# Eight key tiles of the value sums from half-precision parts made by VectorE, on one Trainium2 core

## The reference, cut to what matters

```
B, T, D = 2, 4096, 256; 16 heads of 16
x_norm = layernorm(x) * gamma + beta
q, k = l2_normalize(heads(x_norm @ w_q)), l2_normalize(heads(x_norm @ w_k)); v = heads(x @ w_v)
align = q @ k.T                                           # per batch and head, 4096 x 4096
resonance = 0.5 + 0.5 * tanh((align - 0.27) * 15)
gate_q, gate_k = 0.25 + 0.75 * sigmoid(q . g_q), 0.25 + 0.75 * sigmoid(k . g_k)
fused = (resonance * gate_q[:, None] * gate_k[None, :]) @ v
x = layernorm(x + fused @ w_o + b_o)
h = silu(fp4_linear(x, w_gate)) * fp4_linear(x, w_up)     # hidden width 704, blocks of 16 rounded to a 4-bit grid
x = layernorm(x + fp4_linear(h, w_down))
```

## Time and profile before

| what | value |
|---|---|
| median of three runs | 4383.23 us (4379.05 to 4384.30) |
| the profiled execution's own time | 4378.88 us |
| its span | 4377.1 us |
| TensorE busy, matmuls | 4111.8 us, 94% |
| ScalarE busy | 4017.1 us, 92% |
| VectorE busy | 1561.6 us, 36% |
| GpSimd busy | 159.5 us, 4% |
| DMA | 313.7 MB, mean 72 GB/s |

### The profile page before, as it was taken

How to read it: one execution, slowest core, us unless ns; L and a number is a source line. 1 busy time by engine, 2 the same in 40 slices (tenths; PEclk the granted TensorE clock), 3 DMA queues, 4 the chain that set the end, 5 groups by cost and what they waited for, 6 DMA issues and landing times.

```text
span 4377.1 us, 69385 instructions
## 1 busy us (share of the span) xinstructions
PE 4111.8 (94%) x28776; PEld 1285.9 (29%) x28776; DVE 1561.6 (36%) x4540; ACT 4017.1 (92%) x3271; POOL 159.5 (4%) x120
## 2 busy tenths in 40 slices
PE   7988899999999999999999999999999999999997
PEld 5651222222222222222222222222222222222223
DVE  6754023333333332333233333333333333333236
ACT  4669999999999999999999999999999999999993
POOL 2330000000000000000000000000000000000001
PEclk9999999999999999999999999999999999999998
DMA  4454444344434443444334433443345334433450
GB/s 114 124 129 78 70 76 65 61 68 78 65 63 67 78 68 60 66 78 71 60 63 78 77 55 62 78 78 56 61 78 78 56 61 78 78 59 59 77 83 13
DMA packets 179871, 313.70 MB, mean 72 GB/s; under 512 B 65264, under 2 KB 141808, under 8 KB 154608
## 3 DMA queue, kind: packets, MB, share of 16 engines
q1 hardware_dynamic: 179568, 309.41, 42.1%
HBM read 266.82 MB, written 42.47 MB: 71 GB/s over the span
## 4 chain that ended last, share of the span: by engine, by line
PE 69%; ACT 23%; DVE 4%; issue 3%; DMA 1%; SPq 1%; POOL 0%; POOLq 0%; DVEq 0%; ACTq 0%
PE ps L1268 35%; ACT room L706 22%; PE ps L1258 20%; PE ps L1295 8%; PE ps L1318 4%; DMA m_f<-fused_t 1%; DVE room L858 1%; PE ps L1213 0%; DVE st L812 0%; DVE xnT L848 0%; PE ps L1224 0%; PE ps L1308 0%; DVE sm L773 0%; DVE sm L774 0%; DVE sm L775 0%
## 5 line engine op out<-in xcount | busy, mean ns | idle before, releaser
L706 ACT ACTIVATE room<-ps 128x1024 f32<-128x1024 f32 (+1 forms) x2816 | 3787.1, 1417 | 178.4 <-PE ps L1258 162.2
L1268 PE MATMUL ps<-room,vt 128*32 128x512 f32 x16384 | 2051.2, 601 | 0.0
L1258 PE MATMUL ps<-qs,room 64*128 64x512 f16 x8198 | 1325.9, 383 | 203.7 <-ACT room L706 182.6
L1258 PEld LDWEIGHTS ps<-qs,room 64*128 64x128 f16 x8198 | 310.4, 93 | 1749.5 <-ACT room L706 1123.1
L1268 PEld LDWEIGHTS ps<-room,vt 128*32 128x32 f32 x16384 | 388.1, 108 | 945.3 <-issue 945.3
L1295 PE MATMUL ps<-wguT,m_xqT 128*128 128x352 f32 x960 | 348.2, 485 | 0.0
L967 DVE TENSOR_TENSOR vz<-ps,vz 128x352 f32<-128x352 f32 x120 | 63.0, 525 | 757.7 <-ACT vz L716 757.7
L972 DVE TENSOR_TENSOR vz<-ps,vz 128x352 f32<-128x352 f32 x120 | 63.0, 525 | 595.9 <-PE ps L1295 595.9
L1318 PE MATMUL ps<-wdnT,wqk 128*128 128x256 f32 x720 | 198.9, 404 | 0.6 <-DVE wqk L937 0.6
L1295 PEld LDWEIGHTS ps<-wguT,m_xqT 128*128 128x128 f32 x960 | 162.6, 189 | 105.2 <-issue 54.3
L600 POOL TENSOR_TENSOR m_x<-m_x,bo 128x256 f32<-128x256 f32 x60 | 43.9, 731 | 3876.7 <-DMA m_x<-in_L_attn_x_dram 3876.7
(11 more groups left out here) (172 smaller groups left out, 2198.0 us busy)
## 6 DMA issues: line engine op xcount, KB each, us to landing
room<-k_parts SPq DMA_DIRECT2D x520, 256.0 KB, 9.4
vt<-v_gated SPq DMA_DIRECT2D x65, 1024.0 KB, 17.9
qs<-q_parts SPq DMA_DIRECT2D x520, 32.0 KB, 10.1
gqb<-q_gates SPq DMA_DIRECT2D x256, 64.0 KB, 2.2
...
fused_t<-fs SPq DMA_DIRECT2D x256, 32.0 KB, 1.7
...
```

The lines of the kernel that those rows point to most:

```text
L706: act.activation(res[:, c, o:o + m, :], ps[:, o:o + m, :], ACT.Sigmoid, scale=2 * SHARP / QK_UP ** 2, bias=-2 * SHARP * THRESH).then_inc(b ...
L1258: ins = pe.matmul(ps[:, BANK[n % 2] + i, :], ks[o:o + HROWS, par, h // 2, kt * P:(kt + 1) * P], qs[o:o + HROWS, par, h // 2, :], start=Tru ...
L1268: ins = pe.matmul(ps[32 * h:32 * h + 32, SUM_BANK, :], vt[:, par, n * HD:n * HD + 32], r, start=kt == 0, stop=kt == KT - 1, skip_group_che ...
```

## The change

Eight of the 32 key tiles, those with kt = 0, 3, 6, 12, 15, 18, 21 and 24, are no longer summed in full precision. VectorE writes a high and a low half-precision part of the resonances of such a tile (`split_results`, two instructions of 2048 columns, after ScalarE's group 4c) and TensorE adds eight half-precision matmuls for it (`split_sums`) at group 4c+4: the stationary operand holds 16 columns of high and 16 of low parts of the values of a head, so that the sums of a head now fill 32 rows, whose halves the output projection adds (`wo` loaded twice, four chunks for two). For this the values are brought to a known scale: stage A keeps their largest magnitude, a chain between the stages turns it into a power of two, and `scale_values` multiplies the values of each unit and makes their parts. Full-precision sums use 16 columns for 32, except key tile 1, which comes first and is padded with zeros. The sums are stored with one DMA of 256 KB for four of 32 KB and loaded with 256 KB for 128 KB; the loads of the query gates move behind them. VectorE's order in a unit interleaves the eight splits with the pieces of the tile's tail; units 0 to 3 have no splits. A unit has 18 loads for 17. The diff, cut to its core:

```diff
-NIN = 2 * 2 * len(PAIRS) + 1
+NIN = 2 * 2 * len(PAIRS) + 2
...
-        at[4 * c + 2] = [0, 1] if c == 0 else [3 * c + 1]
+        at[4 * c + 2] = [1, 0] if c == 0 else [3 * c + 1]
...
+def split_at(n):
+    return [SPLIT.index(c) for c in SPLIT if 4 * c + 4 == n]
...
+SPLIT = [0, 1, 2, 4, 5, 6, 7, 8]
...
+RES_UP = 2.0 ** 12
+V_TOP = 2.0 ** 22
+FIRST_KT = 1
+NST, NFL = 1, 1
...
+def is_split(kt):
+    return kt % 3 == 0 and kt // 3 in SPLIT
...
-WEIGHT_LOADS = 9
+WEIGHT_LOADS = 8 + 2 * HG
...
-A_CHAIN = 14
+A_CHAIN = 16
...
-    fd = nc.dram_tensor("fused_t", [B, D, T], F32).ap()
+    fd = nc.dram_tensor("fused_t", [B, 2 * D, T], F32).ap()
...
-        wo = sb("wo", [P, DC, D])
+        wo = sb("wo", [P, NG, D])
...
-        vt = sb("vt", [P, 2, KT * HG * HD + HD])
+        vt = sb("vt", [P, 2, KT * HG * HD])
...
+        vp = carve(wtmp, 64, [2, HG, 2 * HD])
...
+        vh = carve(xT[:, :, :].rearrange("p c n -> p (c n)"), 0, [2, NSPLIT, HG * 2 * HD], FP16)
...
+        r_hi = [carve(wgu_flat, 1024 * i, [HG * BLK], FP16) for i in range(2)]
+        r_lo = [carve(a, 0, [HG * BLK], FP16) for a in (wdn_flat, xnT_flat)]
...
-        m_f = sb("m_f", [P, DC, P])
+        m_f = carve(wgu_flat, 2048, [NG, P])
...
-            sp.dma_start(wo[:, :, :], rows(w_o)).then_inc(s_w, 16)
...
+            for h in range(HG):
+                for m in range(2):
+                    o = 32 * h + m * HD
+                    sp.dma_start(wo[o:o + HD], w_o.rearrange("(g h d) n -> h d g n", g=NG, h=HG)[h]).then_inc(s_w, 16)
...
+                    if n == NIN - 2:
+                        sp.dma_start(vt[:, par], vd[b, g].rearrange("p k e -> p (k e)")).then_inc(b_in[par], 16)
+                        continue
                     if n == NIN - 1:
-                        sp.dma_start(vt[:, par, 0:KT * HG * HD], vd[b, g].rearrange("p k e -> p (k e)"))\
+                        sp.dma_start(vp[:, par, :, 0:HD],
+                                     vd[b, g, :, FIRST_KT, :].rearrange("p (h d) -> p h d", d=HD))\
                           .then_inc(b_in[par], 16)
                         continue
...
-                for h in range(HG):
-                    sp.dma_start(fd[b, (g * HG + h) * HD:(g * HG + h + 1) * HD, bass.ds(i * BLK, BLK)],
-                                 fs[32 * h:32 * h + HD, :]).then_inc(b_st, 16)
...
+                sp.dma_start(fd[b, g * P:(g + 1) * P, bass.ds(i * BLK, BLK)], fs[:, :]).then_inc(b_st, 16)
...
+            def load_sums(dst, j, t, done):
...
                 b, i = j // QB, j % QB
-                return sp.dma_start(dst, fd[b, :, bass.ds(i * BLK + t * P, P)].rearrange("(c r) t -> r c t", r=P))
+                sp.dma_start(dst, fd[b, :, bass.ds(i * BLK + t * P, P)].rearrange("(g r) t -> r g t", r=P))\
+                  .then_inc(done, 16)
...
-                for h in range(HG):
-                    sp.dma_start(gqb[32 * h:32 * h + 32, :],
-                                 gqd[b, g * HG + h:g * HG + h + 1, bass.ds(i * BLK, BLK)]
-                                 .to_broadcast([32, BLK])).then_inc(b_gq, 16)
                 if begins(j, g):
                     k = u - HG
                     wait(sp, l_r, k)
                     sp.sem_inc(sp_pass, 1)
                     sp.dma_start(m_x[:, :], x_tile[k]).then_inc(l_x, 16)
...
-                    sp.wait_ge(b_st, 16 * HG * u)
+                    sp.wait_ge(b_st, 16 * NST * u)
...
-                    load_sums(m_f[:, :, :], j - 1, g).then_inc(l_f, 16)
+                    load_sums(m_f, j - 1, g, l_f)
+                for h in range(HG):
+                    sp.dma_start(gqb[32 * h:32 * h + 32, :],
+                                 gqd[b, g * HG + h:g * HG + h + 1, bass.ds(i * BLK, BLK)]
+                                 .to_broadcast([32, BLK])).then_inc(b_gq, 16)
...
-            pool.memset(vt[:, :, KT * HG * HD:], 0.0).then_inc(b_ev, 1)
+            pool.wait_ge(s_wdot, DC)
+            pool.memset(vp[:, :, :, HD:], 0.0).then_inc(v_pad, 1)
+            pool.memset(ones, 1.0).then_inc(b_ev, 1)
...
+            after(dve.memset(vmx, 0.0))
...
+            def largest_value():
+                after(dve.tensor_reduce(v_mx, vmx[:, 0:TB], AX_X, ALU.max))
+                dve.tensor_scalar(v_mx, v_mx, 2.0 ** -100, None, ALU.max).then_inc(v_mxd, 1)
+                dve.wait_ge(v_row, 1)
+                after(dve.tensor_reduce(v_one, ps[0:1, C_BANK, 0:P], AX_X, ALU.max))
+                dve.tensor_scalar(v_one.bitcast(I32), v_one.bitcast(I32), EXPONENT, None, ALU.bitwise_and)\
+                   .then_inc(v_oned, 1)
+            def value_scales():
+                dve.wait_ge(v_col, 1)
+                dve.tensor_scalar(v_down, ps[:, C_BANK, P:P + 1], 1 / V_TOP, None, ALU.mult)
+                after(dve.reciprocal(v_up, ps[:, C_BANK, P:P + 1]))
+                after(dve.tensor_scalar(v_up, v_up, V_TOP, None, ALU.mult))
+            def scale_values(u):
+                par, split = u % 2, u >= HG
+                dve.wait_ge(b_in[par], 16 * NIN * (u // 2 + 1))
+                wait(dve, v_pad, 1)
+                ins = dve.tensor_scalar(vp[:, par], vp[:, par], v_up, None, ALU.mult)
+                ins = dve.tensor_scalar(vt[:, par], vt[:, par], v_up, None, ALU.mult)
+                if not split:
+                    ins.then_inc(b_v, 1)
+                    return
+                after(ins)
+                v4 = vt[:, par].rearrange("p (k h d) -> p k h d", k=KT, h=HG)
+                parts = []
+                for i, n in ((0, 3), (3, 5)):
+                    k = 3 * SPLIT[i]
+                    two = vh[:, par, i:i + n].rearrange("p i (h m d) -> p i h m d", h=HG, m=2)
+                    parts.append((v4[:, k:k + 3 * n - 2:3], two[:, :, :, 0], two[:, :, :, 1]))
+                for v, hi, lo in parts:
+                    ins = dve.tensor_scalar(hi, v, 1 / RES_UP, None, ALU.mult)
+                after(ins)
+                for v, hi, lo in parts:
+                    ins = dve.scalar_tensor_tensor(out=lo, in0=v, scalar=1 / RES_UP, in1=hi,
+                                                   op0=ALU.mult, op1=ALU.subtract)
+                ins.then_inc(b_v, 1)
...
+                    after(dve.tensor_reduce(vmx[:, TB:2 * TB], vz[:, par, :, 0:D], AX_X, ALU.max,
+                                            apply_absolute_value=True))
+                    after(dve.tensor_tensor(vmx[:, 0:TB], vmx[:, 0:TB], vmx[:, TB:2 * TB], ALU.max))
+                    if isinstance(n, int) and n == NBLK - 1:
+                        largest_value()
...
+                if isinstance(n, int) and n == NBLK - 1:
+                    value_scales()
+                    scale_values(0)
...
-            def end_transposes(k):
-                for half in range(2):
+            def end_transposes(k, halves=(0, 1)):
+                for half in halves:
                     dve.wait_ge(l_H, 2 * k + half + 1)
                     if half == 0:
...
+            def begin_quantize(k, par):
...
                 wait(dve, l_X, k)
                 to_grid(m_xq[:, :], x1, D, m_xs, m_xn[:, :], m_e[:, :], m_t[:, :]).then_inc(l_xq, 1)
...
-            def gates(k):
+            def turned(k):
                 dve.wait_ge(l_X, k + 1)
                 dve.tensor_copy(m_xqT[:, :, :].rearrange("p c n -> p (c n)"), ps[:, C_BANK, 0:D]).then_inc(l_xT, 1)
-                for p in range(4):
+            def gates(k, pieces):
+                for p in pieces:
...
+            def hidden(k):
                 dve.wait_ge(l_ge, 4 * k + 4)
                 wait(dve, l_H, 2 * k)
                 to_grid(m_hq[:, :], m_hb[:, :], F, q_s[:, 0], q_xn[:, :], q_e[:, :], q_t[:, :]).then_inc(l_hq, 1)
...
-                wait(dve, b_st, 16 * HG * u)
+                wait(dve, b_st, 16 * NST * u)
                 dve.wait_ge(b_pv, (u + 1) * KT)
-                dve.tensor_tensor(fs[:, :], ps[:, SUM_BANK, :], gqb[:, :], ALU.mult).then_inc(b_ev, 1)
+                dve.scalar_tensor_tensor(out=fs[:, :], in0=ps[:, SUM_BANK, :], scalar=v_down, in1=gqb[:, :],
+                                         op0=ALU.mult, op1=ALU.mult).then_inc(b_ev, 1)
...
+            def split_results(u, g, i):
+                n = 4 * SPLIT[i]
+                r = res[:, (NGRP // 2 * g + n // 2) % RES_CYCS, 0:HG, :].rearrange("p h n -> p (h n)")
+                if i >= 2:
...
+                    dve.wait_ge(b_pv, u * KT + SPLIT_POS[i - 2] + 1)
+                dve.wait_ge(b_act, u * NGRP + n + 1)
+                after(dve.tensor_scalar(r_hi[i % 2], r, RES_UP, None, ALU.mult))
+                dve.scalar_tensor_tensor(out=r_lo[i % 2], in0=r, scalar=RES_UP, in1=r_hi[i % 2],
+                                         op0=ALU.mult, op1=ALU.subtract).then_inc(b_cv, 1)
...
-                if ends(j, g):
-                    end_transposes(u - HG - 1)
                 if begins(j, g):
-                    begin_tile(u - HG, g % 2)
-                if ends(j, g):
-                    end_tile(u - HG - 1, (g - 1) % 2)
```

(60 more changed lines are left out.)

37 lines of the change are left out of this document (28 added, 9 removed).

## The result

| | before | after |
|---|---|---|
| median of four runs each, side by side | 4383.72 us (4379.05 to 4384.30) | **4477.67 us** (4475.09 to 4481.81) |
| span of the profiled execution | 4377.1 us | 4473.3 us |
| mean granted TensorE clock | 0.995 | 0.992 |

The changed kernel takes 1.0218 times as long [1.0200, 1.0235]. The forecast was 4520 with a range of 4430 to 4620. The direction and the range held; the forecast is 42 us too high, and the pieces show where.

The account below looks back on a forecast made before the run. The prediction took the coupling of TensorE and ScalarE, busy 95% and 96% in the units, as the bound. 4378.9 + 35 outside the units + 60 x 1.7 = 4516, the median 4.3 higher: 4520 us, range 4430 to 4620.

Parts of the forecast that it names:

- The six places named: ScalarE idles in a unit at groups 10, 14, 15, 34, 38, 39: 0.95, 0.4, 0.7, 0.3, 0.25, 0.75 us.
- Units: The 60 units with splits: each becomes 64.0 us, plus 1.7.
- The wait for split 3: In a unit, VectorE ends split 3 at 32.4, TensorE wants it at 31.3; later groups come 0.95 us later.
- The walk without that wait: Group-by-group walk of TensorE and ScalarE through a unit: 63.0 us, plus 0.7, although work was removed.
- Stage A: Its loop through VectorE and ScalarE's cast has no slack; the new reduction adds 22 us over 15 steps.
- The term of 1.47 a step: Stage A: reduction (1.22), maximum (0.16) and gaps stand before ScalarE's cast, 1.47 us in each of 15 steps.
- Start, transition, tail: Outside the units: more load issues at the start 3.6 us, scale chain before first scores 7, four tail tiles 2.5.
- The 0.38-us rounds: Rival on TensorE: each half-precision round costs a whole matmul, 0.38 us, a split 0.77; 4620 us, chance 0.05.
- the 4620: Total in us if a pack of column-grouped half-precision matmuls takes one matmul's duration plus about 4 ns per further tile.
- The full-slope high part: Rival on VectorE: high part at full slope, a split 4.65 us, VectorE becomes the bound; 4660 us, chance 0.07.
- VectorE keeps up: Rival in the units: faster low part or end_tile released earlier, units at 63.0 us; 4460 us, chance 0.25.
- Faster: Rival: removed passes shorten units in full, 2.2 us each, if ScalarE's idle falls under 2.8; 4286 us, chance 0.11.

Follow-up runs that it names:

- experiment 2: Changed kernel with end_tile's normalization moved behind split 3, nothing left out: 4433.76 us, a unit of 62.47 us.
- 1: Changed kernel without stage A's running largest magnitude of the values, a constant in its place: 4443.63 us.
- 6: Changed kernel with stage A's largest-value instructions, last scale and first scaling moved behind `parts(2)`, nothing left out: 4440.74 us.
- experiment 11: Changed kernel with stage A's reduction reading half of the value columns (512 for 1024): 4462.23 us.
- 9: Changed kernel with largest value late, normalization behind split 3, and sums of tiles 9, 11, 27, 29 placed by a recalculated walk: 4350.58 us, 0.9933 of before.
- 12: Kernel with sums placed by the recalculated walk, plus output projection in two pieces and split 2 ahead of `begin_tile`: 4327.62 us, 0.9878 of before.
- 8: Changed kernel with largest value late, tiles 2, 9 and 27 at other groups, and normalization behind split 3: 4432.58 us, a unit of 62.98 us.
- 7: Changed kernel with the full-precision sum of key tile 2 moved from group 4 to group 3: 4503.23 us.
- 5: Changed kernel with full-precision sums of tiles 9 and 27 moved from groups 12 and 36 to 16 and 38: 4460.16 us.

## Why the prediction was right, and where its sizes were off

**Direction: right, by the mechanism given.** TensorE lost work, and the unit grew, because load stands unevenly and ScalarE idles at the hand-overs. The six places named (groups 10, 14, 15, 34, 38, 39) were given 0.95, 0.4, 0.7, 0.3, 0.25 and 0.75; measured 0.87, 0.44, 0.72, 0.33, 0.33 and 0.72.

**Units: plus 0.94 each for plus 1.7, 57 us for 102.** (0.94 is over the 60 units with splits; the lengths of the experiments are means over 63, in which it is 0.90.) This is 45 us too high. Stage A, 9.5 too low, hides part of it, so that the forecast looks better than its pieces: that much is luck. Two terms of the unit were too large, each of the kind forecast.
- The wait for split 3 was put at 1.1, with 0.95 for the unit; it is 0.72 and, by experiment 2, 0.66. The date was missed, as forecast, at the right split alone, but by less, and it was TensorE that moved it. `end_tile` starts when the down projection ends, at 24.3 in the unit where 24.8 stood; from there VectorE needs 7.3 us for 7.6, so that split 3 ended at 31.64 for 32.4; and TensorE wanted it at 30.98 for 31.3. VectorE's load had no part in it, since VectorE idles 1.50 us ahead of that piece.
- The walk without that wait gave 63.0, plus 0.7; experiment 2 has 62.47, plus 0.24. TensorE takes up groups 8, 12 and 16 at 11.76, 17.67 and 23.76, where 12.1, 18.0 and 24.5 stood: the cycles with the projection and with three tiles at group 12 were priced 0.25 and 0.4 too long.

**Stage A: 31.5 for 22.** The loop has no slack and the delay is in front of the cast: right, and experiments 1 and 6 show it. The term of 1.47 a step was mis-sized: the instructions and their gaps take 1.64, the step grew by 2.10. The missing 0.46, 6.9 us in 15 steps, is the clock; experiment 11 finds 7.4 us of it. I had said nothing of the clock in stage A, since TensorE idled only 3.4 us at line 1208 in 288 and had 1.00; the change raised that idle time to 25.9.

**Start, transition, tail:** 1.2 for 3.6 (the load that VectorE waits for landed 4.1 us after its issue for 6.4), 4.4 for 7, 2.2 for 2.5.

**The prices.** Right: high part 1.24 for 1.22, low part 2.29 for 2.28, projection 1.99 busy, 0.44 net for a split on TensorE (a sum with it 1.42 us, a sum alone 0.98), its rounds 0.21 apart. The 0.38-us rounds fall. So does the 4620 that the Trainium skill ("TensorE: Matmul & The Clock Gate", Measured speedup vs the span model) would have given by itself. That figure was also summed too high: half of 8 x 0.33 is 1.3 a unit and not 1.7, so that the rival stands at about 4600, and the upper end of the range with it. The full-slope high part falls, and with it VectorE as the bound: it is busy for 77%. Wrong, but without effect: scaling the values, put at 2.28 from the row with per-partition scalars, took 1.28. That row has two such scalars and the full slope, this instruction one and half. The microsecond gained could only let VectorE wait longer for TensorE, 2.49 us before `begin_tile`.

**The rivals.** "VectorE keeps up" had 4460, and experiment 2 shows that state 26 us lower, 4434, the walk being high. "Faster" fell for this placement, 0.94 on the wrong side for 2.2 on the right one; but its point, that ScalarE's idle time decides, is what 9 and 12 stand on: they bring 0.5 and 0.9 us a unit against before. Its threshold was misread, though. ScalarE idled 2.75 us a unit before (173.5 of 3925 us, 62.97 units), not 3.4, so that "under 2.8" held already; the changed kernel has 4.06.

**Open:** how the 0.77 us a unit that 9 gains on 2 divide between its four moved sums. By ScalarE's gaps it is half and half between tiles 9 and 11 (0.72 to 0.28) and tiles 27 and 29 (0.72 to 0.28), but the kernels move them together. And why 8 loses 0.51 against 2 alone: its gaps have 0.31 more before group 6 (tile 2, as in 7), 0.10 more before group 41 and 0.17 less behind group 15 (tiles 27 and 9, as in 5), which is 0.24; the other 0.27 shows in no gap that I read.
